# Second attention layer: unnormalised exponentials turned, divided behind the value product

## The reference, cut to what matters

```python
q = query @ Wq + bq; k = key @ Wk + bk; v = value @ Wv + bv   # per batch, 16 heads of 16
attn = softmax(einsum('bhqd,bhkd->bhqk', q, k) * SCALE, axis=-1)
out = einsum('bhqk,bhkd->bhqd', attn, v)                      # -> 512 x 256
x = x + tanh(g_xattn[1]) * (out @ Wo + bo)
```

## Time and profile before

| | |
|---|---|
| median of 3 runs | 603.48 us |
| profiled execution | 595.08 us, its span 592.7 us |
| PE busy over the span | 84% |
| DVE busy | 71% |
| ACT busy | 50% |
| POOL busy | 42% |
| mean granted TensorE clock | 0.927 |

### The profile page before, as it was taken

The page is one execution under the profiler, slowest core; times in us unless marked ns, Lnnn a source line. Parts: engine busy times, 40 slices in busy tenths (PEclk is TensorE's granted clock), DMA queues, the critical chain, the costliest instruction groups (busy, mean ns, idle before and its releaser), DMA issues.

```text
span 592.7 us, 10230 instructions
## 1 busy us (share of the span) xinstructions
PE 499.5 (84%) x3061; PEld 364.4 (61%) x3069; DVE 419.2 (71%) x809; ACT 294.2 (50%) x521; POOL 247.1 (42%) x314
## 2 busy tenths in 40 slices
PE   7888899896998699899999999944897777649994
PEld 3456658566784278788888888812553544425562
DVE  6598898787546987494756823227979899588992
ACT  1446555362654466483755623203454444427884
POOL 5454263344300311020212110066367878538996
PEclk9989899699698899899999999979599989588999
DMA  7940100100167156555554310022000000000112
GB/s 212 296 147 1 37 0 2 36 0 1 35 215 236 31 161 221 180 178 168 174 178 154 94 35 18 18 81 71 0 1 1 1 1 1 0 0 2 36 35 71
DMA packets 35162, 46.40 MB, mean 78 GB/s; under 512 B 2764, under 2 KB 25304, under 8 KB 35128
## 3 DMA queue, kind: packets, MB, share of 16 engines
q1 hardware_dynamic: 30856, 39.02, 20.4%
q0 software_dynamic: 1680, 4.59, 2.7%
q10 hardware_dynamic: 2592, 2.36, 1.2%
HBM read 38.36 MB, written 7.60 MB: 78 GB/s over the span
## 4 chain that ended last, share of the span: by engine, by line
PE 45%; DVE 28%; POOL 10%; issue 7%; ACT 3%; DMA 2%; SPq 2%; DVEq 1%; POOLq 0%; ACTq 0%
PE s_tile L976 16%; PE bank L997 8%; DVE s_max L1476 4%; DVE p_sum L1490 4%; PE bank L827 3%; DVE probs L1481 3%; PE bank L986 3%; DVE stats L1414 2%; DVE xn L1436 2%; DVE ew L1436 2%; PE bank L711 2%; PE s_tile L1070 2%; POOL probs_t L614 2%; DMA w<-in_L_xattn_W 2%; DVE ew_lo L1746 2%
## 5 line engine op out<-in xcount | busy, mean ns | idle before, releaser
L506 POOL TENSOR_TENSOR probs<-probs,p_rcp 128x1024 f32<-128x1024 f32 x32 | 60.9, 1907 | 94.3 <-DVE p_rcp L1493 94.3
L740 PE MATMUL bank<-ident,probs 128*128 128x128 f32 x256 | 40.4, 309 | 27.0 <-POOL probs L506 25.3
L976 PE MATMUL s_tile<-ew_hi,xs_hi 128*128 128x512 f32 x144 | 59.9, 416 | 3.7 <-DVE ew_lo L1746 2.5
L1167 ACT COPY probs_t<-bank 128x512 f32<-128x512 f32 x64 | 35.0, 588 | 47.1 <-PE bank L740 46.7
L976 PE MATMUL s_tile<-ew_hi,xs_lo 128*128 128x512 f32 x144 | 57.5, 399 | 0.0
L976 PE MATMUL s_tile<-ew_lo,xs_hi 128*128 128x512 f32 x144 | 57.4, 398 | 0.0
L740 PEld LDWEIGHTS bank<-ident,probs 128*128 128x128 f32 x256 | 32.9, 159 | 39.5 <-POOL probs L506 30.1
L564 POOL TENSOR_TENSOR token_now<-token_of,carried 128x1 uint32<-128x1 uint32 x17 | 3.8, 226 | 124.1 <-PE bank L960 124.1
L1764 DVE TENSOR_TENSOR probs_t<-s_tile,probs_t 128x512 f32<-128x512 f32 x36 | 24.8, 689 | 43.1 <-PE s_tile L976 41.7
L1137 ACT ACTIVATE probs<-probs 128x1024 f32<-128x1024 f32 x32 | 33.9, 1058 | 33.8 <-DVE probs L1481 33.7
L1476 DVE TENSOR_REDUCE s_max<-s_tile 128x16 f32<-128x1024 f32 x32 | 38.4, 1199 | 16.6 <-PE s_tile L724 16.5
(11 more groups left out here) (228 smaller groups left out, 1318.8 us busy)
## 6 DMA issues: line engine op xcount, KB each, us to landing
ew<-in_L_ffn_w SPq DMA_DIRECT2D x32, 512.0 KB, 5.0
ew<-in_L_ffn_w SPq DMA_DIRECT2D x8, 1024.0 KB, 5.7
slots_y<-xn ACTq DMA_DIRECT2D x18, 128.0 KB, 3.9
x_res<-in_x SPq DMA_DIRECT2D x4, 512.0 KB, 6.4
token_rows<-ew SPq DMA_DIRECT2D x4, 512.0 KB, 3.1
out_rows<-x_res SPq DMA_DIRECT2D x3, 512.0 KB, 3.0
w<-in_L_xattn_W SPq DMA_DIRECT2D x2, 512.0 KB, 9.4
ew<-in_L_ffn_w_gate SPq DMA_DIRECT2D x1, 1024.0 KB, 12.9
```

Of the source, the lines that this page charges most:

```text
L506: nc.gpsimd.tensor_tensor(p, p, p_rcp[:, i, :].unsqueeze(2).to_broadcast([P, H, M]), ALU.mult).then_inc(s["p_norm"], 1)
L740: last = nc.tensor.transpose(t_bank[c][:, P * j:P * j + P], probs[:, i % 2, at:at + P], ident[:])
L976: last = nc.tensor.matmul(o[:], x, w, start=(k == 0 and n == 0), stop=(k == DK - 1 and n == 2))
L1167: last = nc.scalar.copy(flat(probs_t[:, i % 2, 4 * c:4 * c + 4, :]), t_bank[c][:])
```

## The change

In the second layer alone, `sums` and POOL's `normalise` go. The exponentials are turned as they are. The value product swaps its operands: the turned exponentials of a head pair (128x128) are loaded and `v_ext` moves, 34 columns: 32 value columns and two columns of ones that give the two heads' sums. It is done per tile, eight products a tile. The output has tokens on partitions; DVE takes the reciprocals of the sums from PSUM and multiplies the 256 outputs into `o_n`; PE turns `o_n` back with two transposes into the same bank; ACT copies to `o_t`. The feed-forward's row norm moves from DVE to POOL (`ff_norm`), with statistics buffers of its own (`ff_stats`, `ff_mv`). Orders on all four engines are new, with a third score tile of the next batch ahead of the border, and the second layer's loops are written out. The first layer's attention is split off with its order unchanged. Helpers keep their bodies (`turn_tile`, `turned_tile` are the former transposes and copies).

```diff
@@ tensors
+VW = 2 * HD + 2
+ff_stats = sb("ff_stats", [P, TB, 6])
+ff_mv = sb("ff_mv", [P, TB, 2])
-v_blk1 = sb("v_blk1", [P, B, PAIRS, 2 * HD])
+v_ext = sb("v_ext", [P, B, PAIRS, VW])
+o_n = flat(h1_t[:, 0:2, :]).rearrange("p (i d) -> p i d", i=TB)
@@ GpSimd
+def ff_norm(b):
+    layer_norm_rstd(pool, ln["ff"], b + 1, ff_mv)
+    pool.wait_ge(ln["ff"]["rstd"], b + 1)
+    carry_wait(2)
+    for i in range(TB):
+        last = nc.gpsimd.tensor_scalar(xn2[:, i, :], x_res[:, TB * b + i, :], ff_mv[:, i, 0:1], rstd[:, i:i + 1],
+                                       ALU.subtract, ALU.mult)
+    last.then_inc(ln["ff"]["xn"], 1)
...
+def second_batch(b):
+    if b:
+        ff_norm(b - 1)
         ff_rows(b - 1)
-    if l == 0 and not last:
-        bias_rows(l, b)
-    if not last:
-        normalise(l, b + 1, 0)
-        if l == 1:
-            centre_rows(b + 2)
-        normalise(l, b + 1, 1)
-        if l == 1:
-            scale_rows(b + 2)
-    layer_norm_rstd(pool, ln["rt" if l == 0 else "ff"], b + 1)
-normalise(0, 0, 0)
-normalise(0, 0, 1)
+    if b + 1 < B:
+        bias_rows(1, b + 1)
+    if b + 2 < B:
+        layer_norm_rstd(pool, ln["l1"], b + 3)
+        centre_rows(b + 2)
+        scale_rows(b + 2)
...
-normalise(1, 0, 0)
-normalise(1, 0, 1)
-batch(1, 0, True, False)
-with pool.Fori(1, B - 1) as b:
-    batch(1, b, False, False)
-batch(1, B - 1, False, True)
+bias_rows(1, 0)
+for b in range(B):
+    second_batch(b)
+ff_norm(B - 1)
@@ TensorE: queries, scores, second_attention
+if not start and l == 1:
+    pe.wait_ge(s["a_o"], TB * n - TB + m + 1)
-if i >= 2 and 0 in chunks:
+if (i >= 2 or l == 1 and n) and 0 in chunks:
...
+def second_attention(b, first_batch, last_batch):
+    s = att[1]
+    def turn(n, i):
+        pe.wait_ge(s["a_exp"], TB * n + i + 1)
+        if i % 2:
+            pe.wait_ge(s["a_pt"], TB * n + i)
+        turn_tile(1, n, i, s["t_pt"])
+    def values(i):
+        pe.wait_ge(s["a_pt"], TB * b + i + 1)
+        if i < 2 and not first_batch:
+            pe.wait_ge(s["v_y"], TB * b - 1 + i)
+        if i >= 2:
+            pe.wait_ge(s["a_o"], TB * b + i - 1)
+        for j in range(PAIRS):
+            last = nc.tensor.matmul(x_bank[i % 2][:, VW * j:VW * j + VW], probs_t[:, i % 2, j, :],
+                                    v_ext[:, b, j, :], start=True, stop=True)
+        last.then_inc(s["t_o"], 1)
+    def turn_back(i):
+        pe.wait_ge(s["v_on"], TB * b + i + 1)
+        for k in range(DK):
+            last = nc.tensor.transpose(x_bank[i % 2][:, P * k:P * k + P], o_n[:, i, P * k:P * k + P], ident[:])
+        last.then_inc(s["t_ot"], 1)
+    def project(i):
+        pe.wait_ge(s["a_o"], TB * b + i + 1)
+        if i == 1 and not first_batch:
+            pe.wait_ge(f["a_x"], b)
+        for k in range(DK):
+            last = nc.tensor.matmul(att_bank[1][i][:, 0:D], o_t[:, k, P * i:P * i + P], wo[:, k, :],
+                                    start=(k == 0), stop=(k == DK - 1))
+        last.then_inc(s["t_y"], 1)
+    if first_batch:
+        scores(1, b, 2)
+        turn(b, 0)
+        scores(1, b, 3)
+        turn(b, 1)
+    values(0)
+    if not last_batch:
+        pe.wait_ge(s["a_pt"], TB * b + 2)
+        turn_rows(1, b + 1)
+    turn_back(0)
+    values(1)
+    turn_back(1)
+    if not last_batch:
+        queries(1, b + 1, first_batch, False)
+    turn(b, 2)
+    if not last_batch:
+        scores(1, b + 1, 0)
+        pe.wait_ge(s["a_q"], DK * b + 2 * DK)
+    values(2)
+    if not last_batch:
+        scores(1, b + 1, 1)
+    turn(b, 3)
+    if not last_batch:
+        scores(1, b + 1, 2)
+    turn_back(2)
+    if not first_batch:
+        pe.wait_ge(s["a_pt"], TB * b + TB)
         ff_turn(b - 1)
+    values(3)
+    for i in range(3):
+        project(i)
+    if not last_batch:
+        pe.wait_ge(s["v_y"], TB * b + 2)
+        turn(b + 1, 0)
+        scores(1, b + 1, 3)
+    turn_back(3)
+    if not last_batch:
+        turn(b + 1, 1)
+    project(3)
@@ ScalarE
+def second_attention(b, first_batch, last_batch):
+    s = att[1]
+    def turned(n, i):
+        if n or i >= 2:
+            act.wait_ge(s["t_o"], TB * n + i - 1)
+        turned_tile(1, n, i)
+    def output(i):
+        act.wait_ge(s["t_ot"], TB * b + i + 1)
+        if not first_batch:
+            act.wait_ge(s["t_y"], TB * b - TB + i + 1)
+        nc.scalar.copy(o_t[:, :, P * i:P * i + P],
+                       x_bank[i % 2][:, 0:D].rearrange("p (k t) -> p k t", k=DK)).then_inc(s["a_o"], 1)
+    if first_batch:
+        turned(b, 0)
+    turned(b, 1)
+    exps(1, b, 2)
+    if not last_batch:
+        turned_rows(1, b + 1)
+    output(0)
+    output(1)
+    if not last_batch:
+        act.wait_ge(s["t_s"], TB * b + TB)
+        queries(1, b + 1)
+    turned(b, 2)
+    exps(1, b, 3)
+    if last_batch:
+        nc.scalar.activation(carried[:, 10 + 2 * TB:11 + 2 * TB], carried[:, 2:3], ACT.Silu)
+    turned(b, 3)
+    output(2)
+    if not first_batch:
+        ff_rows(b - 1)
+    if not last_batch:
+        exps(1, b + 1, 0)
+        exps(1, b + 1, 1)
+        turned(b + 1, 0)
+    output(3)
@@ VectorE: scores, preparation, second_attention
-if i >= 2:
+if i >= 2 or l == 1 and n:
...
+for half in range(2):
+    nc.vector.memset(v_ext[half * M:half * M + M, :, :, 2 * HD + half:2 * HD + half + 1], 1.0)
...
+def second_attention(b, first_batch, last_batch):
+    s = att[1]
+    def normalise(i):
+        g = TB * b + i
+        o = x_bank[i % 2][:, 0:VW * PAIRS].rearrange("p (j v) -> p j v", j=PAIRS)
+        rcp = p_rcp[:, i, :].rearrange("p (j h) -> p j h", j=PAIRS)
+        dve.wait_ge(s["t_o"], g + 1)
+        nc.vector.reciprocal(rcp, o[:, :, 2 * HD:VW]).then_inc(s["v_rcp"], 1)
+        dve.wait_ge(s["v_rcp"], g + 1)
         if not first_batch:
+            dve.wait_ge(s["t_ot"], g - TB + 1)
+        nc.vector.tensor_tensor(o_n[:, i, :].rearrange("p (j h a) -> p j h a", j=PAIRS, h=2),
+                                o[:, :, 0:2 * HD].rearrange("p j (h a) -> p j h a", h=2),
+                                rcp.unsqueeze(3).to_broadcast([P, PAIRS, 2, HD]),
+                                ALU.mult).then_inc(s["v_on"], 1)
+    def add_rows(i):
+        g = TB * b + i
+        dve.wait_ge(s["t_y"], g + 1)
+        nc.vector.scalar_tensor_tensor(row(g), att_bank[1][i][:, 0:D], tg[:, 1:2], row(g), ALU.mult,
+                                       ALU.add).then_inc(s["v_y"], 1)
+        if last_batch:
+            dve.wait_ge(s["v_y"], g + 1)
+            row_stats(ln["ff"], TB * b, (i,), ff_stats)
+    normalise(0)
+    if not first_batch:
+        dve.wait_ge(s["v_y"], TB * b)
+        row_stats(ln["ff"], TB * b - TB, range(TB), ff_stats)
+        join_stats(ln["ff"], b, ff_stats, ff_mv)
+    normalise(1)
+    if first_batch:
+        add_experts(GATHERS[3][TB:])
+    if b + 2 < B:
+        if b:
+            dve.wait_ge(p_xm, b)
+        join_stats(ln["l1"], b + 3)
+    scores(1, b, 3)
+    if not first_batch:
+        row_scales(b - 1)
+    if not last_batch:
+        scores(1, b + 1, 0)
+    normalise(2)
+    if not last_batch:
+        scores(1, b + 1, 1)
+    normalise(3)
+    dve.wait_ge(s["p_xb"], b + 1)
+    for i in range(3):
+        add_rows(i)
+    if not last_batch:
+        scores(1, b + 1, 2)
+    if b + 3 < B:
+        dve.wait_ge(g_x, NT)
+        row_stats(ln["l1"], TB * b + 3 * TB)
+    add_rows(3)
+    if last_batch:
+        join_stats(ln["ff"], B, ff_stats, ff_mv)
@@ VectorE, before the attention
-sums(1, 0, 0)
 scores(1, 0, 1)
+scores(1, 0, 2)
 dve.wait_ge(g_y[3], 16 * len(GATHERS[3]))
 add_experts(GATHERS[3][:TB])
-sums(1, 0, 1)
-add_experts(GATHERS[3][TB:])
-dve.wait_ge(g_x, NT)
-attention(1, 0, True, False)
-with dve.Fori(1, B - 1) as b:
-    attention(1, b, False, False)
-attention(1, B - 1, False, True)
+dve.wait_ge(g_x, GATHERS[3].start + TB)
+row_stats(ln["l1"], 2 * TB)
+for b in range(B):
+    second_attention(b, b == 0, b == B - 1)
@@ VectorE, in the feed-forward's first tile
-norm_apply(ln["ff"], B, NT - TB, xn2)
```

More of the change, by code:

```diff
@@ L728, in scores, with turn_tile, first_attention @@
                     last.then_inc(s["t_s"], 1)
-            def attention(l, b, first_batch, last_batch):
-                s = att[l]
+            def turn_tile(l, b, i, turned):
+                for c in range(2):
+                    for j in range(4):
+                        at = P * (j // 2 * 4 + 2 * c + j % 2)
+                        last = nc.tensor.transpose(t_bank[c][:, P * j:P * j + P], probs[:, i % 2, at:at + P], ident[:])
+                    last.then_inc(turned, 1)
+            def first_attention(b, first_batch, last_batch):
+                s = att[0]
                 def turn(i):
@@ L852, in attention, with first_product @@
-                pe.wait_ge(s["v_y"], TB * b + 2)
+                if not last_batch:
+                    scores(0, b + 1, 1, (1,))
+                if first_batch:
+                    pe.wait_ge(p_wlo, 4)
+                def first_product(m, cols):
```

(27 more changed lines are left out.)

322 lines of the change are left out of this document (131 added, 191 removed).

## The result

The change made the kernel slower: 602.92 us median of 20 runs (599.76 to 612.74), against 598.62 us of 20 runs of the kernel before on the same chip, ratio 1.0094 [1.0067, 1.0121] (in brackets the 95% interval). In a later comparison the same kernel gave 1.0026 [0.9981, 1.0071], which is not apart from no change. The ratios leave out runs more than 1.5% above the fastest run of the same kernel, while the medians hold them, and the two profiles of the changed kernel (611.49 and 608.08 us) are both of such longer runs. I had forecast 598.3 from 603.5, 5.2 us less. That 602.92 lies inside my range of 594 to 603 is luck: 603.48 was the median of three runs, and 20 runs gave 598.62, from where my step leads to 593.4, 9.5 us under the measured median.

The account below looks back on a forecast made before the run. DVE bounded the batch before, PE after: 96.1 us work plus 11.8 waits against 111.5 gives -3.6; feed-forward -1.9 and fills +0.3 make -5.2, so 603.5 becomes 598.3 us, range 594 to 603.

Parts of the forecast that it names:

- the router's row: Second attention's value products, priced by the router's product with the same 128x128 load: 1.88 us a tile, 7.5 a batch.
- the waits in sum: PE's waits left by the written order: 3.6 us first batch, 1.6 middle batches, 6.6 last batch; 11.8 with all.
- My list of works and waits: PE's work and waits from first subtraction to the feed-forward's first product: 96.1 + 11.8 = 107.9 us, against 111.5 before.
- the 96.1 us of PE's work: Second attention after the change: turns, scores, values, turns back, queries, projections and feed-forward turns on PE, together 96.1 us.
- the clock counts fully: PE, now the bound, would feel its clock fully; no term in the sum, only a rival adding 14 us.
- the first rival: Half clock from `values(0)` to mid-queries each batch adds 3.5 us, 14 in all: 612 us, slower; chance 0.25.
- like its own rounding: Feed-forward row norm moved to POOL, four operations priced as its rounding: 0.47 us each, 1.9 a batch.
- the 1.9 us promised in the feed-forward: DVE's 2.90 us last-batch norm leaves the path of the first feed-forward tiles for POOL: 1.9 us won.
- the first batch's wait: First batch: `scores(3)` waits for the second subtraction because VectorE puts a row norm between: 1.7 us.
- a middle batch at full clock: Second attention's middle batch: 25.8 us of PE work and 0.8 of wait, 26.6 against 26.4 before.
- the cheaper value products: Value products at 1.14 instead of 1.88 us a tile: 586.5 us; chance 0.25, together with larger gains at the ends.
- the third: Waits on PE's order keep DVE the bound; middle stays 26.4 us, total 601.6; shares the forecast's 0.50 chance.

Follow-up runs that it names:

- added products: Changed kernel with dummy bf16 products of 512 columns filling TensorE's waits, in the first batch and before each turn back: 601.86 us, ratio 1.0074.
- changed again: The changed kernel unaltered, measured again beside the others on one chip: 603.47 us median of 12, ratio 1.0026.
- queries split: Changed kernel with the first half of the next batch's queries placed ahead of the second turn back: 601.44 us, ratio 1.0081.
- norms on DVE: Changed kernel with the feed-forward's row norm back on VectorE for all four batches, GpSimd keeping its short statistics: 600.96 us, ratio 1.0033.
- the kernel of all repairs: Changed kernel with bias addition behind first-batch statistics, feed-forward row norms on VectorE, queries split and last batch reordered: 603.35 us, ratio 1.0015.
- the bf16 kernels: Changed kernel with second-layer turned exponentials and values in bf16: 584.68 us, ratio 0.9732; the same with all repairs of order: 577.15 us, ratio 0.9643.

## Why the prediction was wrong

**Right.** DVE was the bound: taking its sums alone away is worth 14.5 us (584.68 against 599.21). The value products cost what the router's row gave, 1.71 to 1.91 us from start to start at full clock for 1.88; DVE's product 0.42 and reciprocal 0.26 came out as taken. In a middle batch PE became the bound, idle only before the second turn back, 0.81 for 0.8.

**Right by luck:** the waits in sum. The rows by stretch give 5.35 + 0.81 + 0.81 + 4.24 = 11.2 us of idle PE, against 11.8. But the first batch has 5.35 for 3.6 and the last 4.24 for 6.6, because there products at half clock fill what would be waits. With added products, at a mean clock of 0.76, the same batch has 7.4 us of idle PE.

My list of works and waits splits by batch into 29.5 + 3.6, twice 25.8 + 0.8, and 14.9 + 6.6. Beside it the measured batches, in us, with the mean granted clock:

| kernel, profiled run | first | middle | middle | last |
|---|---|---|---|---|
| forecast | 33.1 | 26.6 | 26.6 | 21.5 |
| changed, 611.49 us | 41.04 (0.79) | 27.34 (0.94) | 27.32 (0.94) | 27.64 (0.63) |
| changed again, 608.08 us | 41.12 (0.79) | 25.63 (1.00) | 25.63 (1.00) | 27.45 (0.63) |
| added products, 600.39 us | 32.64 (1.00) | 25.69 (1.00) | 25.69 (1.00) | 28.47 (0.76) |
| queries split, 603.91 us | 34.70 (0.95) | 25.52 (1.00) | 25.52 (1.00) | 28.79 (0.64) |
| norms on DVE, 600.92 us | 34.74 (0.95) | 27.25 (0.94) | 27.28 (0.94) | 22.82 (0.78) |

**Wrong: the 96.1 us of PE's work, taken at full clock.** The step that failed is "the clock counts fully" without a price for it in the sum. The four attention stretches hold 112.1 us of busy PE (35.69 + 26.53 + 26.51 + 23.40), 16.0 more. Their clocks mean, at two levels, 17.2 + 3.3 + 3.3 + 20.5 = 44.3 us at half clock. What that costs differs by batch:

- First: in the kernel with norms on DVE this batch has the changed kernel's order on every engine, and takes 34.74 us at 0.95 where the changed kernel took 41.04 at 0.79. So 6.3 of the 7.9 us over the forecast go with the clock, in this execution.
- Middle: 1.7 us each where the clock is 0.94, nothing where it is 1.00.
- Last, up to `ff_turn`: nothing. It starts 16.57 us into the batch in the changed kernel (527.88 - 511.31), where the clock is at half from 4 us in on, and 16.57 us into it with added products (516.30 - 499.73), where it is at full for 12 us. There the chain over POOL's norm and DVE's row scales sets the time.
- Last, behind `ff_turn`: 11.07 and 11.90 us in these two, at half clock, against 7.84 with norms on DVE (528.77 - 520.93), where the clock is back at full, and 7.6 in my list. So 3.5 to 4.3 us are clock. In the kernel before, too, this part ran at half clock, the 16 projection records in 5.54 us, and I took them at full.

I put the clock into the first rival at 0.25 and spread it evenly over the batches. It sits in the first and at the end of the last, and the first batch's part follows the execution. Over the whole kernel the changed kernel's runs go from 599.84 us at a mean clock of 0.928 to 610.8 at 0.905, those of the kernel before from 591.95 at 0.932 to 603.69 at 0.909. The kernel before pays ahead of this stage, whose start moves from 402.95 to 407.04 us as the clock up to there goes from 0.94 to 0.92. The mean clock of the two kernels is the same, 0.923 and 0.922 in one comparison.

The rule that the prediction drew on, in the Trainium skill, "TensorE: Matmul & The Clock Gate", "Part 4: PE-mode transpose", that transposes don't count as PE activity, is neither borne out nor refuted: no run isolates them, and a middle batch with all its turns stood at 1.00 in one profile and at 0.94 in the other.

**Wrong: POOL's norm.** Priced "like its own rounding", 0.47 us a tile, it takes 1.215. The two have the same 256 columns, but the norm has two operands per partition (mean and factor) where the rounding has one; that this is the reason was not isolated. A nearer row stood in the trace of before: POOL centres and scales the rows of a batch in two operations of 1.90 and 1.89 us, 3.8 together, where I took 1.9 for the norm:

```profile
L512 POOL TENSOR_TENSOR xn<-x_res,mv 128x1024 f32<-128x1024 f32 x3 | 5.7, 1895 | 0.0
```

In the last batch the norm delays the row scales and the turned rows: `ff_turn` starts at 16.57 us where my list has 13.9, and at 14.98 with norms on DVE (520.93 - 505.95). Of the 1.9 us promised in the feed-forward nothing came: 70.75 us against 70.0, and 70.9 with that batch's norm back on DVE. How the two costs of the last batch, norm and clock, depend on each other is not shown: the kernel of all repairs has its norms on DVE too, though another order in this batch, and took 28.50 us with the clock at half to the end; 22.82 stands in the one profile with no norm on POOL and the clock back at full behind `ff_turn`.

**Wrong: the first batch's wait**, 1.7 forecast and 3.63 found, because POOL's bias addition, moved to the stage's start, runs beside DVE's norm and stretches it from 1.38 to 3.33 us. I had counted what the moved step costs on its own queue, not what it does to its neighbour.

**Too dear:** a middle batch at full clock, 25.6 for 26.6. This hid a part of the errors.

No profile shows a run of the changed kernel near its median. An estimate from the table for one, 34.7 + 25.6 + 25.6 + 28 = 114 us, is 3 us over the 111.5 of before, with 0.3 to 0.9 us more in the feed-forward; the ratios say 1.6 to 5.6 us. By it most of the miss in such a run is the last batch, and the 6 us that half clock costs in the first batch belong to the longer runs. This fits the added products, which held the clock in the first batch and shortened only the longest runs.

Of the rivals, the cheaper value products did not come, and the third, DVE staying the bound, is refuted by 18 us of 25.6. Why the clock falls where it does stays open. Taking a wait away and filling it each kept the first batch at full clock in a profile, but no pair of kernels separates this in time, and the last batch fell in every profile, the bf16 ones too. Whether the bf16 kernels gain by the missing 1.5 us a tile alone, or partly since less work is exposed to the clock, was not separated either; 16 x 1.51 = 24 us at full clock is the most that the tiles can give, and the stage fell by 20.8 from 128.1.

## What to carry over

When a change moves the bound from one engine to another, price the new bound at the clock that the old trace shows there, not at full clock: low clock that waits covered under the old bound can be paid for under the new one. Then look stretch by stretch at what still covers it: here the first batch paid, and the last, up to `ff_turn`, did not, since GpSimd held it. Price an operation by a row that does the same work, not by one with the same column count, and ask of every moved step what runs beside it. And before giving up a change whose idea is sound, ask which single term ate it; here it was two 128-column f32 loads per product, and rounding the operands of that one product to bf16 turned a ratio of 1.003 to 1.009 into 0.973.

## What was not expected of the hardware

- VectorE's reciprocal scales steeply: 0.26 us for 16 columns, 1.744 for 256, where a product of 256 is 0.425.
- VectorE beside GpSimd: four operations of 256 columns in 3.33 us next to a 1,024-column addition of GpSimd, 1.38 without it.
- GpSimd's operation with two operands per partition: 1.215 us for 256 columns, 0.47 for another one with one.
- Eight value products in bf16, 128 columns loaded and 34 moving: 0.36 us against 1.87 in f32, a factor of 5 and not the 2 of the record count. The Trainium skill, "TensorE: Matmul & The Clock Gate", "Weight-path perf modes — Fast Weight Load (FWL) and DoubleRow", says that loads of 128 weights are read in a faster way when their type is not FP32. This trace agrees.
- In f32, 32 records with 32 columns loaded and 128 moving take about 0.9 us, 0.03 each; with 128 loaded and 34 moving it is 1.87/16 = 0.12 each.
